# An adaLN transformer block on one core: two loads moved to ACT's queue, fewer matmuls of zeros, and an affine ahead of low parts

## The reference

```python
mod = (silu(c) @ wmod).reshape(2, 6, 1, -1)        # six vectors per batch: sa, ca, ga, sb, cb, gb
ga, gb = sign(g) * max(|g|, 0.25)
h = layernorm(x) * (1 + ca) + sa
Q, K, V = split(h @ c_attn_w + c_attn_b)
base_A  = softmax(Q[:, :128] @ K[:, :128].T * 0.25)
cam     = tanh((base_A @ V[:, :128]) * cam_gate) @ K[:, :128].T
attn    = softmax(Q @ K.T * 0.25 + cam * 0.25 * sigmoid(w0 + 0.5 * w1))
x = x + ga * ((attn @ V) @ c_proj_w + c_proj_b)
h = layernorm(x) * (1 + cb) + sb
x = x + gb * (gelu(h @ proj1.T + proj1_bias) @ proj2.T + proj2_bias)
```

## Time and profile before

| | |
|---|---|
| median of 3 runs | 322.36 us |
| profiled execution | 322.67 us |
| its span, first to last instruction | 320.9 us |
| PE busy | 313.8 us, 98% |
| DVE busy | 214.3 us, 67% |
| ACT busy | 157.6 us, 49% |
| POOL busy | 108.5 us, 34% |
| DMA | 10.31 MB, mean 32 GB/s |

### The profile page before, as it was taken

How to read it: one execution, slowest core, us unless ns; L and a number is a source line. 1 busy time by engine, 2 the same in 40 slices (tenths; PEclk the granted TensorE clock), 3 DMA queues, 4 the chain that set the end, 5 groups by cost and what they waited for, 6 DMA issues and landing times.

```text
span 320.9 us, 5227 instructions
## 1 busy us (share of the span) xinstructions
PE 313.8 (98%) x2022; PEld 283.9 (88%) x2022; DVE 214.3 (67%) x415; ACT 157.6 (49%) x266; POOL 108.5 (34%) x131
## 2 busy tenths in 40 slices
PE   8889999999999999999999999999999999999996
PEld 6778989888999998898899888898999999899895
DVE  5695689996555669886743789898664575753531
ACT  2465575563334337816932486545532244860930
POOL 4431755154445656135011132140021232603311
PEclk9999999999999999999999999999999999999999
DMA  7920030600000000000001000000000000001001
GB/s 219 375 64 1 0 67 1 239 24 0 3 0 2 0 2 1 2 33 33 3 22 43 2 1 2 0 2 0 0 2 0 2 0 2 0 3 50 16 7 62
DMA packets 8025, 10.31 MB, mean 32 GB/s; under 512 B 704, under 2 KB 6592, under 8 KB 8000
## 3 DMA queue, kind: packets, MB, share of 16 engines
q1 hardware_dynamic: 8000, 9.98, 9.4%
HBM read 7.35 MB, written 2.10 MB: 29 GB/s over the span
## 4 chain that ended last, share of the span: by engine, by line
PE 86%; DVE 9%; ACT 3%; issue 2%; DVEq 0%
PE a_ps L190 13%; PE a_ps L189 13%; PE a_ps L188 13%; PE s_ps L188 11%; PE s_ps L190 11%; PE s_ps L189 11%; PE t_ps L1096 7%; DVE nmax L750 2%; PE s_ps L938 2%; PE t_ps L1023 2%; DVE k_lo L720 1%; PE s_ps L953 1%; DVE th L732 1%; DVE q_hi L718 1%; ACT prob L524 1%
## 5 line engine op out<-in xcount | busy, mean ns | idle before, releaser
L514 ACT ACTIVATE pt_hi<-t_ps 128x512 fp32r<-128x512 f32 x64 | 35.0, 596 | 67.6 <-PE t_ps L1096 67.5
L750 DVE TENSOR_REDUCE nmax<-s_ps 128x1 f32<-128x1024 f32 x32 | 39.0, 1220 | 14.9 <-PE s_ps L190 14.9
L524 ACT ACTIVATE prob<-s_ps,nmax 128x1024 f32<-128x1024 f32 x32 | 35.8, 1119 | 13.3 <-DVE nmax L750 13.1
L744 DVE TENSOR_TENSOR pt_lo<-t_ps,pt_hi 128x512 fp32r<-128x512 f32 x64 | 40.9, 681 | 1.3 <-ACT pt_hi L514 1.3
L188 PE MATMUL s_ps<-k_hi,q_hi 128*128 128x512 f32 x96 | 38.4, 400 | 0.2 <-DVE k_lo L671 0.2
L344 POOL TENSOR_SCALAR prob<-prob,rinv 128x1024 f32<-128x1024 f32 x16 | 18.0, 1127 | 58.3 <-DVE rinv L754 58.3
L190 PE MATMUL s_ps<-k_hi,q_lo 128*128 128x512 f32 x96 | 37.7, 393 | 0.0
L189 PE MATMUL s_ps<-k_lo,q_hi 128*128 128x512 f32 x96 | 37.5, 391 | 0.0
L188 PE MATMUL a_ps<-v_hi,pt_hi 128*128 128x256 f32 x128 | 36.8, 288 | 0.0
L188 PE MATMUL a_ps<-w_hi,pt_hi 128*128 128x256 f32 x128 | 36.4, 284 | 0.0
L189 PE MATMUL a_ps<-w_lo,pt_hi 128*128 128x256 f32 x128 | 36.2, 283 | 0.0
(11 more groups left out here) (150 smaller groups left out, 760.6 us busy)
## 6 DMA issues: line engine op xcount, KB each, us to landing
w_raw<-w_t SPq DMA_DIRECT2D x2, 1024.0 KB, 6.2
out<-x_all SPq DMA_DIRECT2D x16, 128.0 KB, 1.7
x_all<-x SPq DMA_DIRECT2D x4, 256.0 KB, 4.8
wmod_raw<-wmod SPq DMA_DIRECT2D x1, 1024.0 KB, 8.5
x_all<-x SPq DMA_DIRECT2D x2, 512.0 KB, 10.3
wmod_raw<-wmod SPq DMA_DIRECT2D x1, 512.0 KB, 4.8
wattn_raw<-w_attn SPq DMA_DIRECT2D x1, 512.0 KB, 6.0
gates<-h SPq DMA_DIRECT2D x4, 128.0 KB, 2.6
```

Source lines behind the costliest of these rows:

```text
L514: A(pt_hi[:, (u // 2) % 2, 4 * g:4 * g + 4, (u % 2) * P:(u % 2 + 1) * P], t_bank(b, "p", 2 * u + g)[:, :].rearrange("p (t n) -> p t n", n= ...
L524: A(prob[:, u % 3, :], s_ps[u % 2][:, :], ACT.Exp, bias=nmax[:, u:u + 1], accum_out=rsum[:, u:u + 1]).then_inc(exp_ready, 1)
L744: V.tensor_tensor(pt_lo[dst], t_bank(b, "p", 2 * u + g)[:, :].rearrange("p (t n) -> p t n", n=P), f(pt_hi[dst]), ALU.subtract).then_inc(pt ...
L750: V.tensor_reduce(nmax[:, u:u + 1], s_ps[u % 2][:, :], AX.X, ALU.max, negate=True).then_inc(nmax_ready, 1)
```

## The change

Three things are edited.

The loads: x's second pair of tiles and the small columns are now issued by ACT, as the first two instructions of its list, in this order. SP's list loses both, and each load behind them moves up. The helper `load_x` takes the engine as an argument.

The zeros: `warm_up` runs six matmuls and not nine, and the memset fills the 256 columns that these read, not 512.

The order on ACT and DVE in the second half of batch 0: the affines `h_high(3)`, `h_high(2)`, `h_full(2)`, `h_full(3)` and the low parts `h_low(3)`, `h_low(2)` now stand ahead of the high and low part of the second value tile (`v_high(0, 1)`, `v_low(0, 1)`), and the low part of the second QK job, `qk_low(1)`, stands behind the third value tile's. TensorE's list and POOL's have no other change than the zeros.

```diff
+        def load_x(eng, i, t, n):
+            eng.dma_start(x_all[:, t:t + n, :], x_v[:, t:t + n, :]).then_inc(x_in[i], 16)
...
         @block.sync
         def _(sp):
-            load_x(0, 0, 2)
-            sp.dma_start(cols_sb[:, :], cols).then_inc(cols_in, 16)
-            load_x(1, 2, 2)
+            load_x(sp, 0, 0, 2)
             sp.dma_start(wmod1_raw[:, :, :], wm[:, :, 0:2 * E]).then_inc(wmod1_in, 16)
...
         @block.scalar
...
+            load_x(act, 1, 2, 2)
+            act.dma_start(cols_sb[:, :], cols).then_inc(cols_in, 16)
             act.wait_ge(cols_in, 16)
...
             qk_high(1)
-            v_high(0, 1)
             h_high(3)
             h_high(2)
+            v_high(0, 1)
             v_high(0, 2)
...
         @block.vector
...
-            V.memset(f32s[:, 0, :], 0.0).then_inc(warm_ready, 1)
+            V.memset(f32s[:, 0, 0:2 * P], 0.0).then_inc(warm_ready, 1)
...
             qk_low(0)
             v_low(0, 0)
-            qk_low(1)
-            v_low(0, 1)
             h_full(2)
             h_full(3)
             h_low(3)
             h_low(2)
+            v_low(0, 1)
             v_low(0, 2)
+            qk_low(1)
...
         @block.tensor
...
-            warm_up(9)
+            warm_up(6)
```

More of the change, by code:

```diff
@@ L260, in _ @@
         def _(sp):
-            def load_x(i, t, n):
-                sp.dma_start(x_all[:, t:t + n, :], x_v[:, t:t + n, :]).then_inc(x_in[i], 16)
             wa = w_attn.rearrange("(c p) n -> p c n", p=P)
             wm = wmod.rearrange("(c p) n -> p c n", p=P)
-            load_x(0, 0, 2)
-            sp.dma_start(cols_sb[:, :], cols).then_inc(cols_in, 16)
-            load_x(1, 2, 2)
+            load_x(sp, 0, 0, 2)
             sp.dma_start(wmod1_raw[:, :, :], wm[:, :, 0:2 * E]).then_inc(wmod1_in, 16)
@@ L273, in _ @@
             sp.dma_start(wp_raw[:, :, :], wp.rearrange("(c p) n -> p c n", p=P)).then_inc(wp_in, 16)
-            load_x(2, 4, 2)
-            load_x(3, 6, 2)
+            load_x(sp, 2, 4, 2)
+            load_x(sp, 3, 6, 2)
             sp.dma_start(wattn_raw[:, :, 2 * E:3 * E], wa[:, :, 2 * E:3 * E]).then_inc(wv_in, 16)
@@ L279, in _ @@
                 .then_inc(rows_in, 16)
-            load_x(4, T, TH)
-            load_x(5, T + TH, TH)
+            load_x(sp, 4, T, TH)
+            load_x(sp, 5, T + TH, TH)
             sp.wait_ge(gate_floor, 2)
```

## The result

The changed kernel takes 324.78 us (median of 4, 324.70 to 325.45) against 322.36 us before: ratio 1.0072, 95% interval 1.0054 to 1.0090. It is slower, by 0.7%; 320.3 us was forecast. Its profiled execution took 324.70 us, with a span of 322.9 us, 2.0 us more than before.

A forecast was written before the change was run, and what follows sets the result against it. TensorE, busy 98% of the span, was taken as the bound, with gains where the chain leaves it or it does unneeded work. Start 1.35 plus reorder 0.75 gave 2.1 us off, 320.3 us; range 319.5 to 322.0.

The forecast's parts named there:

- The start, zeros: Kernel's opening on TensorE: cutting three matmuls of zeros saves 1.3 us, the shorter memset 0.2; zeros end at about 6.5.
- first rival: Clock's rise needs the cut work; modulation and transposes run at 1.2 GHz, 2.6 us lost, 322.9 us; chance 0.10.
- The start, small columns: Small columns, issued on ACT behind x's pair, land at 4.6 us (3.8 to 6.0), so sct is ready at 6.0.
- The start, second pair's norm: DVE's norm of both x pairs, delayed with sct: xn ends between 8.0 and 8.7 us, before at 7.94.
- second rival: Small columns land at 6.0 or beyond, transposes end near 10.8, the start gains nothing: 321.6 us; chance 0.12.
- The table load: ACT's 1.28 us table load, behind two DMA issues, ends near 3.0, before the columns, and stays hidden.
- The second half's affine: Second half of batch 0: reordered DVE and ACT let TensorE start at 21.4 instead of 22.16, 0.75 us gained (0 to 1.01).
- third rival: Reorder gains nothing, as DVE and ACT slow each other's bank reads or k_lo ends behind k_hi: 321.0 us; chance 0.09.
- Shifts arrive whole from 26 us on: From 26 us on, order and durations are unchanged, so the 2.1 us of earlier gains reach the end whole.

The follow-up runs named there:

- POOL later: Changed kernel with small columns ahead of x's second pair on ACT, two zeros behind the transposes, and POOL's wqk_lo waiting for all four xn: 322.02 us.
- zeros in the modulation: Changed kernel plus one matmul of zeros behind each of the first three of the modulation's four groups of matmuls: 326.86 us, ratio 1.0079.

## Why the prediction was wrong, point by point

**The start, zeros: the step that failed.** The text took three matmuls of zeros as work "that nobody needs" and booked 1.3 us of gain. It had the clock as its first rival, with 0.10, and set it aside because "the zeros that go came after the rise and can't have caused it". That is true of the rise and beside the point: with the cut zeros gone the clock did not stay up through the modulation and the transposes. The runs: zeros alone, 0 of 10 executions at full clock and 1.7 us slower; with the order but without the loads, 0 of 8; the changed kernel itself, 0 of 8; and in the profiles of these the clock falls between 8.05 and 10.05 us, in the modulation, in the transposes or between them. The rival foresaw no rise; what happened is a rise and then a fall. Its price, 2.6 us lost, was close to the 2.46 us measured (0.55 plus 1.91) by luck: it priced the modulation and eight transposes, of which only four transposes ran at half clock, and most of the loss lay in the projections behind them, which it only mentioned. The rest of its 322.9 us was off mainly because it also booked the 1.35 us gain of the start, which did not come.

The rule of the Trainium skill that the text cited ("TensorE: Matmul & The Clock Gate", Part 1) says that activity releases the half clock, and it spoke against the change. The text used its scatter of the rise, for 0.25 us, and not its other side, that idleness brings the half clock back. The trace agrees that it comes back, 0.50 from 10.05 to 16.9; but the idle stretches ahead of it were short, 0.39 us and the 0.6 us from 9.45 on.

**The start, small columns: mis-sized.** Taken at a landing of 4.6 us, bounds 3.8 and 6.0; measured 5.5. sct was ready at 6.90, not 6.0. The loads on SP were as forecast: the modulation's weights were issued at 1.21, with 4.5 us to landing, so there at about 5.7 (taken 6.1). The wait for weights became a wait for columns. (The 1,047 KB of the text should be 1,035 KB in the profile's units; the ends at 4.7 and 6.8 hardly move.)

**The start, second pair's norm: not foreseen.** xn was to end between 8.0 and 8.7 and ended at 10.39. Of this the late columns are one part, since DVE's reciprocal stands ahead of the second pair's statistics; the other is 0.9 us by which POOL's wqk_lo slows the two xn when they overlap. In the kernel before wqk_lo came behind them (9.56 against 7.94), so no row showed the collision. At full clock the loads alone cost 0.6 us instead of giving anything, though with nine zeros in front they had little to give; with six, the modulation started at 7.04 with them and at 6.92 without. The second rival, late columns, is close to what happened here: it had the transposes end near 10.8 and the start gain nothing, and at full clock they would have ended at about 11.0. But its condition, columns at 6.0 or later, wasn't met; the collision, which no rival had, made up for it.

**The table load** stayed hidden behind two issues: 1.76 to 3.04, well ahead of 5.5. Right.

**The second half's affine.** 0.75 us forecast, 0.61 from the trace, and 0.52 (at full clock) to 0.67 us (all executions) from the order alone: right in kind, the size a little high. The 0.35 us of room on DVE was 0.43. The third rival, that the reorder gains nothing, is refuted.

**Shifts arrive whole from 26 us on.** Right: 73.80 us in both traces, with busy times equal to 0.03 us.

Still open is what about the missing zeros lets the clock fall. Two causes go together in these runs: the work that is gone, and the short idle stretches that the cut opens. Every profiled execution in which the clock fell had TensorE idle somewhere between the zeros and the fall (0.74 us in all with zeros only, about 0.35 us with POOL later), and so had one in which it held (0.49 us, zeros in the modulation). No gap at one fixed place is needed; that some gap is needed isn't excluded. A run with six zeros and no idle time at all would be needed. Open too is why the loads lower the clock even with nine zeros.

## What to carry to other kernels

Before matmuls of zeros are cut, look at what TensorE does for the next several microseconds: if it is matmuls of two columns, transposes and waits, the zeros may be holding the clock, and their price must be set against what every matmul costs at 1.2 GHz. A busy share of 1.00 is no assurance: with zeros only the clock fell under one. When a load is moved to a second queue, ask who stands second on it: in this case either the small columns or an x pair took 1.6 us longer to land than on the one queue. And compare several executions with their granted clocks, since one profile shows one of several outcomes.

## What the runs showed of the hardware

- The granted clock fell under an unbroken row of busy TensorE instructions (zeros only: busy 0.50 of 0.50 us, clock 0.99 and then 0.50), when these were matmuls of two columns and transposes. The row had lasted 2.1 us by then, behind 0.74 us of idle time.
- The column of the granted clock prints 1.00 from 1.2 to 6.6 us, where the spacing of the zeros shows 1.2 GHz; later it prints 0.50 for the same speed. At the start of a kernel the record spacing has to be read instead.
- Two of DVE's tensor_scalar of 128x256 took 1.62 us beside POOL's tensor_tensor and 0.73 alone; POOL's two took 1.46 us against 1.42. The loss is almost all on DVE. The Trainium skill, "SBUF — State Buffer", "Terms", has both engines arbitrate for one pair of ports, where the loser blocks and doesn't share; the trace agrees in kind, for the slowed xn end 0.14 us behind POOL's pair (10.39 and 10.25).
- An 11 KB load took 2.6 us to land behind 256 KB on SP's queue and 4.25 us behind 256 KB on ACT's, with the weights flowing on SP's at the same time.
- The executions of the kernel before lay within 0.06 us on one chip (322.30 to 322.36) and between 321.58 and 325.89 us on another, where the mean granted clock separates the long ones: 0.989 in the two at 325.9, 0.995 in four from 323.26 to 324.52. Among the 25 at full clock it doesn't: the four at 0.998 took 321.58 to 322.26 and the thirteen at 1.00 took 322.26 to 323.01. The column misses the half clock at the start, so it can't show how early the clock rose.
